# Seven of 36 probability tiles per group turned through memory instead of on TensorE, in a pre-norm attention and LoRA block

## The reference

```python
x = x + attention(layernorm(x))     # 32 query heads, 8 key/value heads, head size 128, causal
x = x + lora_ffn(layernorm(x))      # 8 experts of rank 16, gated by a softmax
# attention, per batch and key/value head, with its 4 query heads:
q, k, v = rmsnorm(x @ Wq.T), rmsnorm(x @ Wk.T), x @ Wv.T
p = softmax(q @ k.T / sqrt(128) + slope * (key - query), causal)
out += (p @ v) @ Wo.T
```

## Time and profile before

| | |
|---|---|
| median of 3 runs | 2156.0 us (2156.0 to 2157.36) |
| profiled execution: its time, its span | 2155.97 us, 2154.1 us |
| PE busy | 2122.3 us of the span |
| DVE, ACT, POOL busy | 1359.1, 1145.4, 787.0 us |
| mean granted TensorE clock | 0.998 of full |
| DMA | 118.01 MB, mean 55 GB/s |

### The profile page before, as it was taken

One profiled execution on the slowest core, in us unless ns is written; L12 is line 12 of the kernel. 1 busy time (PEld: TensorE's weight loads), 2 busy tenths in 40 slices (PEclk: granted clock), 3 DMA queues, 4 the chain that ended last, 5 costly groups with the idle time before them and its releaser, 6 DMA issues.

```text
span 2154.1 us, 33327 instructions
## 1 busy us (share of the span) xinstructions
PE 2122.3 (99%) x12220; PEld 1825.0 (85%) x12220; DVE 1359.1 (63%) x3431; ACT 1145.4 (53%) x3314; POOL 787.0 (37%) x872
## 2 busy tenths in 40 slices
PE   7999999999999999999999999999999999999997
PEld 6888888888888888888888888888888888888885
DVE  6566665666565666668765656565565656566676
ACT  4555555565555655555545555554555555555552
POOL 3343333334333442334333334242432424244341
PEclk9999999999999999999999999999999999999999
DMA  5121200212102120112120111111011111101101
...
DMA packets 32128, 118.01 MB, mean 55 GB/s; under 512 B 4184, under 2 KB 4184, under 8 KB 23776
## 3 DMA queue, kind: packets, MB, share of 16 engines
...
q10 hardware_dynamic: 432, 0.01, 0.0%
...
## 4 chain that ended last, share of the span: by engine, by line
PE 97%; DVE 1%; ACT 1%; issue 0%; DMA 0%; POOL 0%; SPq 0%; POOLq 0%; DVEq 0%; ACTq 0%
PE s_ps L926 19%; PE o_ps L926 18%; PE turn_ps L1013 17%; PE y_ps L926 17%; PE q_ps L926 16%; PE turn_ps L926 9%; PE y_ps L1082 1%; PE turn_ps L1007 1%; DMA wkv_raw<-in_L_attn_Wv 0%; DVE oT_lo L851 0%; ACT oT_hi L662 0%; DVE pT_lo L810 0%; SPq L555 0%; ACT pT_hi L634 0%; DVE y L857 0%
## 5 line engine op out<-in xcount | busy, mean ns | idle before, releaser
L719 POOL TENSOR_TENSOR probs<-probs,p_inv 128x896 f32<-128x896 f32 (+7 forms) x512 | 578.5, 1151 | 690.3 <-DVE p_inv L830 690.2
L634 ACT ACTIVATE pT_hi<-turn_ps 128x512 fp32r<-128x512 f32 x576 | 339.5, 598 | 357.2 <-PE turn_ps L1013 357.0
L810 DVE TENSOR_TENSOR pT_lo<-turn_ps,pT_hi 128x512 fp32r<-128x512 f32 x576 | 391.0, 686 | 206.7 <-ACT pT_hi L634 204.5
L823 DVE CUSTOM_DVE_ANT_0 probs<-s_ps,rel 128x896 f32<-128x896 f32 (+7 forms) x512 | 383.0, 752 | 188.3 <-issue 187.1
L641 ACT ACTIVATE probs<-probs,neg_max 128x640 f32<-128x640 f32 (+7 forms) x512 | 397.3, 778 | 157.0 <-DVE neg_max L823 155.9
L1013 PE MATMUL turn_ps<-ident,probs 128*128 128x128 f32 x2336 | 342.9, 273 | 7.7 <-DVE probs L750 7.6
L1013 PEld LDWEIGHTS turn_ps<-ident,probs 128*128 128x128 f32 x2336 | 286.9, 141 | 71.7 <-issue 10.7
L926 PE MATMUL s_ps<-kT_hi,qT_hi 128*128 128x512 f32 (+3 forms) x768 | 273.5, 356 | 1.0 <-DVE qT_lo L812 0.4
L926 PE MATMUL s_ps<-kT_hi,qT_lo 128*128 128x512 f32 (+3 forms) x768 | 262.7, 342 | 0.0
L926 PE MATMUL s_ps<-kT_lo,qT_hi 128*128 128x512 f32 (+3 forms) x768 | 262.0, 341 | 0.0
L926 PE MATMUL o_ps<-pT_hi,v_hi 128*128 128x512 f32 x576 | 246.9, 429 | 1.2 <-DVE oT_lo L851 1.0
...
## 6 DMA issues: line engine op xcount, KB each, us to landing
wq_raw<-in_L_attn_Wq SPq DMA_DIRECT2D x8, 1024.0 KB, 11.7
wq_kept<-wqT_hi SPq DMA_DIRECT2D x8, 1024.0 KB, 3.9
wq_kept<-wqT_lo SPq DMA_DIRECT2D x8, 1024.0 KB, 7.7
wo_raw<-in_L_attn_Wo SPq DMA_DIRECT2D x8, 1024.0 KB, 10.0
wo_kept<-woT_hi SPq DMA_DIRECT2D x8, 1024.0 KB, 5.3
wo_kept<-woT_lo SPq DMA_DIRECT2D x8, 1024.0 KB, 7.3
wqT_hi<-wq_kept SPq DMA_DIRECT2D x8, 1024.0 KB, 4.8
wqT_lo<-wq_kept SPq DMA_DIRECT2D x8, 1024.0 KB, 6.9
```

What stands on the lines that cost most here:

```text
L634: nc.scalar.activation(target, bank, ACT.Copy).then_inc(sems["high"], 1)
L719: nc.gpsimd.tensor_tensor(row, row, p_inv[:, s % 2, h:h + 1].to_broadcast((P, L)), ALU.mult).then_inc(sems["normalise"], 1)
L810: nc.vector.tensor_tensor(target, bank, upper.bitcast(F32), ALU.subtract).then_inc(sems["low"], 1)
L823: nc.vector.tensor_tensor_reduce(out=probs[:, s % 2, h, 0:L], in0=s_ps[:, at_col:at_col + L], in1=rel[:, S - L:S], scale=-float(slopes[w % ...
```

## The change

**Seven tiles of a group are no longer turned on PE.** They are j = 5 of row block 5, j = 5, 6 of row block 6 and j = 4 to 7 of row block 7. In the first batch and in the second this is the same; 16 groups give 112 tiles. For such a tile:

- `send_p.s.h` (SP, one DMA for each of the 4 heads) writes the head's part of these tiles from `probs` to the memory buffer `p_bounce`, once `normalise.s.h` is done. Runs are of 512 B.
- `fetch_p.s.j` (SP) waits until all four sends have landed, and until the `p_raw` buffer (there are two) is free, that is until `lower_p` of the fetch two before is done. It then issues 4 DMAs, one for each 32 partitions. They bring the tile back with its 32x32 blocks at their transposed places, in runs of 32 numbers (128 B), 2048 runs per tile.
- `flip_p.s.j` (DVE) waits for the landing and transposes the 32x32 blocks in place.
- `upper_p.s.j` (ACT) copies to `pT_hi`, and `lower_p.s.j` (POOL) subtracts for `pT_lo`. `values.s.j` (PE) waits for that instead of `low.p`.

These tiles' `values` come last in their row block. The `turn.p`, `high.p` and `low.p` of these tiles are gone. `pT_hi` and `pT_lo` have 2 slots for tiles turned on PE and 2 for those from memory, where there were 3 for all.

**Room and loads.** To make room in SBUF, the raw Wq and Wo share one buffer (`w_raw`), so `load_wq` now waits for `turn.wo.3` of the group before and `load_wo` for `turn.wq.3`; the small FFN tables load into `f_x`; `probs` for even row blocks is 896 wide.

**New lists.** All six lists are written anew. All their other items are the same work in another order.

```diff
+MEMORY_TILES = {5: (5,), 6: (5, 6), 7: (4, 5, 6, 7)}
...
-    "turn.wo.0 turn.wo.1 high.wo.0 norm_q.1 scores.0.0 high.wo.1 turn.wo.2 max.0.0 scores.0.1 low.wo.0 exp.0.0 q.2.0 "
...
+    "q.8.2 high.p.6.1 keep_wo values.6.0 low.p.6.1 exp.7.2 scores.7.3 invert.7.0 normalise.7.0 turn.p.6.2 max.7.3 "
+    "values.6.1 high.p.6.2 normalise.7.1 send_p.7.0 q.8.3 low.p.6.2 fetch_p.6.6 exp.7.3 turn.kv.1 invert.7.1 "
...
+    TURN_SLOTS, MEMORY_SLOTS, RAW_TILES = 2, 2, 2
...
+            def send_p(w, s, h):
+
+                first = through_memory(s)[0]
...
+                after(sp, "normalise", w, s, h)
+                sp.dma_start(p_bounce[s % 2, first:s + 1, h].rearrange("u p c -> p u c"),
+                             probs[s % 2][:, h, first * P:(s + 1) * P].rearrange("p (u c) -> p u c", c=P)).then_inc(p_sent[s % 2], 16)
+
+            def fetch_p(w, s, j):
+
+                n = fetch_number[w, s, j]
+                sp.wait_ge(p_sent[s % 2], sent[w, s])
+                if n >= RAW_TILES:
+                    after(sp, "lower_p", *p_fetch[n - RAW_TILES])
+                blocks = p_bounce[s % 2, j].rearrange("h (a i) (b j) -> b i (h a) j", i=BLOCK, j=BLOCK)
+                for b in range(NBLK):
+                    sp.dma_start(p_raw[b * BLOCK:(b + 1) * BLOCK, n % RAW_TILES, :].rearrange("p (n j) -> p n j", j=BLOCK),
+                                 blocks[b]).then_inc(p_fetched[n % RAW_TILES], 16)
...
+            def upper_p(w, s, j):
+                after(act, "flip_p", w, s, j)
...
+            def lower_p(w, s, j):
+                r = p_slot[w, s, j]
+                after(pool, "upper_p", w, s, j)
...
+            def flip_p(w, s, j):
+                n = fetch_number[w, s, j]
+                dve.wait_ge(p_fetched[n % RAW_TILES], 16 * NBLK * (n // RAW_TILES + 1))
+                raw = p_raw[:, n % RAW_TILES, :]
+                nc.vector.transpose(raw, raw).then_inc(sems["flip_p"], 1)
...
-                after(pe, "low", "p", w, s, j)
+                if j in through_memory(s):
+                    after(pe, "lower_p", w, s, j)
+                else:
+                    after(pe, "low", "p", w, s, j)
```

More of the change, by code:

```diff
@@ L300, in attention_lora_block, with through_memory, values_order @@
         plans.setdefault(w, group_a if w < NG else group_b)
+    def through_memory(s):
+        return list(MEMORY_TILES.get(s, ()))
+    def values_order(s):
+        return [j for j in range(s + 1) if j not in through_memory(s)] + through_memory(s)
     def ffn_batch(w):
@@ L338, in attention_lora_block @@
             number[named(w, *item)] = counted[item[0]]
+    p_slot, p_before, p_fetch, sent = {}, {}, [], {}
+    turned, flipped, sends = [], [], [0, 0]
+    for w in range(-1, LAST_W + 1):
+        for item in plans[w]:
+            if item[:2] == ("turn", "p"):
+                p_slot[(w, *item[2:])] = len(turned) % TURN_SLOTS
+                turned.append((w, *item[2:]))
+            elif item[0] == "flip_p":
+                p_slot[(w, *item[1:])] = TURN_SLOTS + len(flipped) % MEMORY_SLOTS
+                p_before[(w, *item[1:])] = flipped[-MEMORY_SLOTS] if len(flipped) >= MEMORY_SLOTS else None
+                flipped.append((w, *item[1:]))
+            elif item[0] == "send_p" and item[2] == G - 1:
+                sends[item[1] % 2] += 16 * G
+                sent[w, item[1]] = sends[item[1] % 2]
+            elif item[0] == "fetch_p":
+                p_fetch.append((w, *item[1:]))
+    fetch_number = {name: n for n, name in enumerate(p_fetch)}
     def follow(work):
@@ L455, in attention_lora_block @@
         sems = {kind: sem(f"{kind}_done") for kind in counted}
+        p_sent = [sem("p_sent_even"), sem("p_sent_odd")]
+        p_fetched = [sem(f"p_fetched{i}") for i in range(RAW_TILES)]
         ident_ready = sem("ident_ready")
@@ L497, in load_wkv @@
                         after(sp, "turn", "wkv", g - 1, 1)
-                    sp.dma_start(wkv_raw[:, 0, :], wk_v[g]).then_inc(wkv_loaded, 16)
-                    sp.dma_start(wkv_raw[:, 1, :], wv_v[g]).then_inc(wkv_loaded, 16)
+                    sp.dma_start(w_raw[:, G, :], wk_v[g]).then_inc(wkv_loaded, 16)
+                    sp.dma_start(w_raw[:, G + 1, :], wv_v[g]).then_inc(wkv_loaded, 16)
             def load_wq(w, *first):
-                g = 0 if first else w + 2
-                if g < NG:
-                    if not first:
-                        after(sp, "turn", "wq", g - 1, C - 1)
-                    sp.dma_start(wq_raw[:], wq_v[g]).then_inc(wq_loaded, 16)
-            def load_wo(w, *first):
                 g = 0 if first else w + 1
@@ L512, in load_wo @@
                         after(sp, "turn", "wo", g - 1, G - 1)
-                    sp.dma_start(wo_raw[:], wo_v[g]).then_inc(wo_loaded, 16)
+                    sp.dma_start(w_raw[:, 0:G, :], wq_v[g]).then_inc(wq_loaded, 16)
+            def load_wo(w, *first):
+                g = 0 if first else w + 1
+                if g < NG:
+                    after(sp, "turn", "wq", g, C - 1)
+                    sp.dma_start(w_raw[:, 0:G, :], wo_v[g]).then_inc(wo_loaded, 16)
             def keep_wkv(w):
@@ L549, in back_wo @@
                 sp.dma_start(woT_lo[:].rearrange("p c n -> p (c n)").bitcast(F32), wo_kept[g, 1]).then_inc(wo_back, 16)
+            def send_p(w, s, h):
+                first = through_memory(s)[0]
+                before = [name for name in sent if name[1] % 2 == s % 2 and sent[name] == sent[w, s] - 16 * G]
+                if before and h == 0:
+                    after(sp, "flip_p", *before[0], through_memory(before[0][1])[-1])
+                after(sp, "normalise", w, s, h)
[10 more added lines that the diff above has]
+                                 blocks[b]).then_inc(p_fetched[n % RAW_TILES], 16)
             def load_y(w, t):
@@ L598, in high @@
                 if of == "p":
-                    target = pT_hi[:, piece(*which) % RING, :]
+                    target = pT_hi[:, p_slot[w, *which], :]
                 elif of == "q":
@@ L760, in low @@
                     plain = f_logits[:, which[0] % 2, :]
+                    if which[0] >= 2:
+                        after(dve, "f_low", ffn_batch(w), which[0] - 2)
                 elif of == "lora":
@@ L786, in low @@
                 if of == "p":
-                    r = piece(*which) % RING
+                    r = p_slot[w, *which]
                     target, upper = pT_lo[:, r, :], pT_hi[:, r, :]
@@ L873, in f_norm @@
                     after(dve, "turn", "logits", 0, NT - 2 + t)
+                else:
+                    after(dve, *(("turn", "b") if t else ("sort_b", NG - 1)))
                 after(dve, "f_rstd", b, t)
@@ L941, in turn @@
                     s, j = which
-                    if j == 0:
+                    if j == values_order(s)[0]:
                         after(pe, "normalise", w, s, G - 1)
-                    sources = [probs[:, s % 2, h, j * P:(j + 1) * P] for h in range(G)]
+                    sources = [probs[s % 2][:, h, j * P:(j + 1) * P] for h in range(G)]
                 elif of == "q":
@@ L956, in turn @@
                         pe.wait_ge(wkv_loaded, 32 * (w + 2))
-                    sources = [wkv_raw[:, m, c * P:(c + 1) * P] for c in (2 * which[0], 2 * which[0] + 1) for m in range(2)]
+                    sources = [w_raw[:, G + m, c * P:(c + 1) * P] for c in (2 * which[0], 2 * which[0] + 1) for m in range(2)]
                 elif of == "wq":
@@ L960, in turn @@
                         pe.wait_ge(wq_loaded, 16 * (w + 2))
-                    sources = [wq_raw[:, h, which[0] * P:(which[0] + 1) * P] for h in range(G)]
+                    sources = [w_raw[:, h, which[0] * P:(which[0] + 1) * P] for h in range(G)]
                 elif of == "wo":
@@ L964, in turn @@
                         pe.wait_ge(wo_loaded, 16 * (w + 1))
-                    sources = [wo_raw[:, c, which[0] * P:(which[0] + 1) * P] for c in range(C)]
+                    sources = [w_raw[:, c, which[0] * P:(which[0] + 1) * P] for c in range(C)]
                 elif of == "x":
@@ L1053, in values @@
             def values(w, s, j):
-                if j == 0:
+                order = values_order(s)
+                if j == order[0]:
                     if s == 0:
```

75 lines of the change are left out of this document (43 added, 32 removed), and 479 rows, old and new, of tables (BOUNDARY, FIRST_B, GROUP_A, GROUP_B).

## The result

The changed kernel takes 2193.99 us (median of 4 runs, 2191.61 to 2196.92) against 2156.42 us (4 runs, 2156.0 to 2157.36): ratio 1.0175, 95% interval 1.0162 to 1.0188. It is slower by 38 us. I had forecast slower by 154 us: the direction was right and the size four times too large. Runs in which the chip granted a low clock from end to end are left out everywhere; there was one, a run of experiment 7 (2974.78 us at a mean granted clock of 0.654, the other three at 0.97).

The account below looks back on a forecast made before the run. TensorE was taken to bound the kernel. 2155.97 us plus 108 (first-batch groups), 23 (other nine) and 24 (clock) gave 2311, said as 2310; the forecast's own range was 2200 to 2400, the range given 2150 to 2440.

Parts of the forecast that it names:

- Removed: Turns of 112 tiles leave TensorE, 0.437 us each: 48.9 us less, alone giving 2107 us.
- Other engines: Flips on VectorE (0.69 us), upper parts on ScalarE (0.60), lower parts on GpSimd (1.05) cost only latency, about 2.4 us.
- Per tile that is 3.7 (5.1) us. I take 3.7: Fetch of one tile, 2048 runs at 29 (40) ns: 3.7 us, range 0.7 to 5.1; 5.2 us to landing, queue empty.
- the 19 times of a rearranged plain DMA: Rival, chance 0.03: the strided fetch bounds everything, 13 us per tile; 2900 us.
- the prediction's clock: Places in us from a group's start, by adding up TensorE's work ahead of each item; new GROUP_A gives 128.1 us.
- whole shift: First-batch group: late fetches stall TensorE 18.5 us in all, less 3.1 saved, so 15.4 us longer.
- six of these in a first-batch chain: Rival of slower fetches, chance 0.10: 5.1 us per tile, six tiles per first-batch chain, 8.4 us more per group; 2420 us.
- The signs: Expected in the trace: changed group lengths, new TensorE and VectorE waits, slow stores and fetches; fast ones would refute the prediction.
- The queue is served in order: On SP's one queue, small transfers wait for large ones ahead: a 256 KB load took 9.3 us instead of 2.7.
- The other nine groups: Groups after w = 6: 5.6 us of stalls against 3.1 saved, so 2.5 us each, 23 us.
- The clock: TensorE's granted clock drops after each group's last stall: 1.5 us per group, 24 us in all.
- The rival "hidden transfers": Chance 0.18: transfers hidden, gain kept, 2107 to 2150 us; gone if fetch (7,4) is issued over 4 us late.

Follow-up runs that it names:

- experiment 7: Also written e7: the changed kernel with eight DMAs of 32 KB per fetch in place of four of 64 KB; 2286.76 us.
- e4: The changed kernel without the sends and fetches, flips and values working on a constant; 2106.61 us.
- e1: The changed kernel with five large weight transfers of the first batch's list moved out from among the late sends and fetches; 2115.49 us.
- e2: The changed kernel with only keep_wq (2 MB) moved behind the last fetch of its first-batch group; 2157.14 us.
- e8: The changed kernel with only keep_wkv and keep_wo (3 MB) moved to the first half of the first-batch group; 2165.1 us.
- e6: The changed kernel with weight loads and keeps issued from ScalarE's queue, sends and fetches staying on SP; 2200.97 us.
- e9: e1 with, in the second batch's list, the flip of (5,5) placed behind low.p.5.3 and low.p.5.4; 2112.13 us.
- e10: e1 with eight DMAs per fetch instead of four; 2199.57 us.

## Why the prediction was right on the direction and wrong on the size

The measured 2194 us lies in the range that I gave (2150 to 2440), but below the forecast's own 2200 to 2400.

**Removed: right.** 48.9 us, 2107 forecast, 2106.61 measured (e4).

**Other engines: right that they cost nothing.** A flip takes 0.71 us (0.69 taken), an upper part 0.63 (0.60). A lower part takes 1.37 us on average (1.05 taken), which is hidden too.

**The step that failed: "Per tile that is 3.7 (5.1) us. I take 3.7".** The term for the fetch, 29 ns per 128 B packet from the FFN table's window, was twice too large. In the changed kernel's window 852.6 to 857 us only fetches ran (0.41 MB, all in packets under 512 B):

```profile
DMA packets 3306, 0.41 MB, mean 93 GB/s; under 512 B 3306, under 2 KB 3306, under 8 KB 3306
...
q1 hardware_dynamic: 3306, 0.41, 59.0%
```

0.59 x 16 x 4.4 us are 41.5 engine-us, 12.6 ns for each of 3306 packets, so 1.6 us per tile. SP's four issues, 1.9 us, are longer, and set the pace: the engines were not full. I had not costed issuing at all. From first issue to flip it is 3.8 us, not 5.2. The 29 ns row had 256 B runs mixed with long packets, and dividing what was left among the short ones loaded all error on them. In the two microseconds of that window that hold nearly all of the short packets (972 to 974 us of the kernel before) stands

```profile
DMA packets 1115, 0.57 MB, mean 287 GB/s; under 512 B 992, under 2 KB 992, under 8 KB 1115
...
q1 hardware_dynamic: 1115, 0.57, 113.0%
```

and the same division gives 22 ns there instead of 29. What is left between 22 and 12.6 ns no run explains: the runs are twice as long, and their layout is another. The Trainium skill ("DMA: Bandwidth & Descriptors", Why small descriptors are slow) led to an estimate of 18 ns and about 2200 us, much nearer than mine; the measured packet, 12.6 ns, is shorter still, and what in fact sets a tile's 1.9 us is the issuing. Its other rule, the 19 times of a rearranged plain DMA (same page, Rules for kernel authors), doesn't show here: with 128 B runs a 64 KB part lands in 2.3 us, and a tile takes 1.9 us where that rival had 13.

What this did to the chain, on the prediction's clock for w = 5:

| step | forecast | measured |
|---|---|---|
| flip (6,6) begins | 108.5 | 102.8 |
| first stall, `values.6.4` | 5.6 | 0.9 (0.6 on average) |
| from `keep_wkv`'s issue to the last send's landing | 31.5 | 25.3 |
| last send lands | 122.5 | 115.0 |
| from first issue of fetch (7,4) to its flip | 5.2 | 3.8 |
| whole shift | 18.5 | 8.5 (7.9 + 0.6), and 2.4 by the clock |

The 6.2 us in the third row are two terms. From 827 to 853 us the queue held 8.33 MB and 92.0% of the engines:

```profile
DMA packets 7276, 8.33 MB, mean 320 GB/s; under 512 B 3689, under 2 KB 5737, under 8 KB 6761
...
q1 hardware_dynamic: 7273, 8.30, 92.0%
```

That is 23.9 us of all 16. At 12.6 ns the 3689 short packets are 2.9 us of it, where my sum has 7.1 for what was left of fetch (6,5) and for fetch (6,6). The rest, sends and weights alike, is 21.0 us for 7.9 MB. Counted in MB of 1024 KB, as the prediction does, that is 7.5 MB and 2.8 us per MB; I had 23.7 us for it: 2.9 per MB of weights, which was nearly right, and 1.2 for a send, which is 0.7 at that rate. (Between the queue's end and a landing my sum put 0.5 and 0.7 us, for which it had no row.) Behind `turn.kv.3` TensorE doesn't wait again; the next flip begins 2.3 us after the first, and the later tiles keep up.

Experiment 7 tells how much of the miss this term carried. With the tile at 3.8 us by its issues the time is 2287 us, where the forecast with 3.7 was 2310: 93 of the 117 us between forecast and result come back. The groups behind the first batch then stand at +7.6 us (w = 7 to 9; 12 forecast) and +27.0 (w = 10 to 14; 20 forecast), so that part of the reckoning holds. The first batch stands at +93.3 of 118.5 forecast. The 25 us missing there are no test of my packet price, since eight DMAs move the same short packets as four: in e7 too the last send lands 26.5 us after `keep_wkv`'s issue, 31.5 forecast. And "six of these in a first-batch chain" was wrong: 1.9 us more per tile made such a group 5.1 us longer (144.25 less 139.2), not 11.

**Where it was right.** `turn.kv.3` behind `low.kv.2` behind the flip of (7,4) is the very wait named; the late last send is its cause (e1, e2, e8).

**The signs.** I had named 147 and 130 us for the groups (139.2 and 124.55), about 20 us of VectorE's waiting for DMAs per first-batch group (16), stores landing in 10 us or more (7.3 here, 8.6 at the most) and fetches in 5 to 9 (2.3 for a DMA at the median, 3.8 from a tile's first issue to its flip). "A fetch in 3 us" I had named as a sign of being wrong, and it came near that.

**The queue: right in effect, wrong in kind.** "The queue is served in order" gave the right delay, but a second queue doesn't help (e6): what is under way on the engines counts, whichever queue it came by.

**The other nine groups: wrong sign.** +2.5 forecast, -2.0 to -3.5 measured. At 1.9 us per tile the fetches of the second batch keep up, except for what e9 mended. With 3.8 us (e10) that batch's period is 131.6, 5.0 above before.

**The clock: too little for the first batch, too much for the second.** 2.4 us per first-batch group against 1.5 taken (17 of the 18.8 us), and next to nothing in the second; in all at most 18.8 against 24.

**The rival "hidden transfers"** was judged by the right test, how late fetch (7,4) is (852.59 less 737.6 is 115.0, its place 103.5: 11.5 us late), and its time is what e1 and e9 reach once the large transfers stand elsewhere.
